# The expert loop of an audio-tower kernel: one run over all three shares instead of one run per share

## The reference

```
logits = xf @ Wr + br                       # xf: 8064 x 64, 64 experts
topk_logits, topk_idx = top_k(logits, 2)
gates = softmax(topk_logits)
for e in range(64):
    h = relu(xf @ W1[e] + b1[e])            # 64 -> 128
    y = h @ W2[e] + b2[e]                   # 128 -> 64
    out = out + combine[:, e:e+1] * y       # combine: the gates, 0 for other experts
```

## Time and profile before

| | us |
|---|---|
| median of 3 runs | 900.72 (898.73 to 900.98) |
| the profiled execution, its own time | 901.74 |
| its span in the profile | 899.9 |
| PE busy (matrix products) | 520.3 (58%) |
| DVE busy | 571.1 (63%) |
| ACT busy | 330.5 (37%) |
| POOL busy | 595.1 (66%) |
| expert loop, first to last y_copy | 524.2 to 793.3 |

### The profile page before, as it was taken

The page is one execution under the profiler, slowest core; times in us unless marked ns, Lnnn a source line. Parts: engine busy times, 40 slices in busy tenths (PEclk is TensorE's granted clock), DMA queues, the critical chain, the costliest instruction groups (busy, mean ns, idle before and its releaser), DMA issues.

```text
span 899.9 us, 9083 instructions
## 1 busy us (share of the span) xinstructions
PE 520.3 (58%) x2514; PEld 348.0 (39%) x2520; DVE 571.1 (63%) x1180; ACT 330.5 (37%) x622; POOL 595.1 (66%) x393
## 2 busy tenths in 40 slices
PE   4653344675576666667357578868767678720050
PEld 4643111221222222234234367747656567610050
DVE  1697899999999999978256623323223223284258
ACT  2169756466556555433113123323222223200020
POOL 5894699999999999913644645635655365557700
PEclk9857578798887797877568788988998799975575
DMA  7999900000000000000350257776876678211102
GB/s 245 383 160 119 48 1 0 0 0 0 0 1 0 0 0 0 0 0 23 86 142 15 69 162 223 196 206 193 230 212 183 185 213 233 59 41 27 26 1 92
DMA packets 106605, 84.96 MB, mean 94 GB/s; under 512 B 30464, under 2 KB 90240, under 8 KB 106560
## 3 DMA queue, kind: packets, MB, share of 16 engines
q1 hardware_dynamic: 79312, 54.76, 28.2%
q10 hardware_dynamic: 19184, 21.40, 7.7%
q0 software_dynamic: 8064, 8.27, 3.6%
HBM read 57.22 MB, written 33.49 MB: 101 GB/s over the span
## 4 chain that ended last, share of the span: by engine, by line
PE 27%; DVE 26%; issue 16%; POOL 13%; ACT 8%; another core or an unknown queue 8%; SPq 1%; DMA 1%; POOLq 0%; DVEq 0%; ACTq 0%
PE ps L907 11%; POOL x_w L576 7%; POOL w_ring L569 6%; PE ps L894 5%; DVE hh_ring L1422 4%; DVE x_w L1616 2%; DVE hh_ring L1633 2%; PE ps L672 2%; ACT ps L1067 2%; DVE x_w L1606 2%; DVE w_ring L1416 2%; ACT ps L1073 2%; PE ps L736 2%; DVE us_lg L1633 2%
## 5 line engine op out<-in xcount | busy, mean ns | idle before, releaser
L736 PE MATMUL ps<-x_w,ident 128*128 128x512 f32 x252 | 151.6, 760 | 102.5 <-POOL x_w L576 102.5
L626 POOL DMA_INDIRECT sorted_rows<-xp,slot_i x126 | 122.0, 968 | 124.2 <-DVE x_w L1616 42.9
L647 POOL DMA_INDIRECT xt<-expert_out,slot_i x126 | 119.9, 952 | 91.0 <-DVE x_w L1616 52.2
L569 POOL TENSOR_TENSOR w_ring<-xt,bc 128x2016 f32<-128x2016 f32 x32 | 144.7, 4522 | 13.5 <-DVE hh_ring L1422 7.3
L1422 DVE TENSOR_TENSOR_SCAN hh_ring<-ps,w_ring 128x1024 f32<-128x1024 f32 x64 | 145.6, 2275 | 0.1
L576 POOL TENSOR_TENSOR x_w<-hh_ring,bc 128x2016 f32<-128x2016 f32 (+1 forms) x32 | 142.4, 4454 | 0.9 <-PE ps L736 0.9
L736 PEld LDWEIGHTS ps<-x_w,ident 128*128 128x128 f32 x252 | 59.2, 245 | 197.7 <-POOL x_w L576 125.8
L1616 DVE COPY x_w<-ps 128x256 f32<-128x256 f32 x80 | 33.9, 424 | 128.4 <-PE ps L907 63.6
L1073 ACT ACTIVATE ps<-dt_t,a_exp 128x1024 f32<-128x1024 f32 x64 | 71.5, 1117 | 64.2 <-DVE hh_ring L1422 64.2
L1067 ACT ACTIVATE ps<-dt_t,a_exp 128x1024 f32<-128x1024 f32 x64 | 71.5, 1118 | 52.1 <-DVE w_ring L1401 52.1
L1164 ACT ACTIVATE x_w<-ps 128x256 f32<-128x256 f32 x80 | 30.6, 383 | 156.4 <-PE ps L883 95.6
(11 more groups left out here) (209 smaller groups left out, 915.8 us busy)
## 6 DMA issues: line engine op xcount, KB each, us to landing
dt_t<-packed SPq DMA_DIRECT2D x140, 96.5 KB
x_w<-packed SPq DMA_DIRECT2D x112, 96.5 KB
x_w<-sorted_rows ACTq DMA_DIRECT2D x40, 256.0 KB
expert_out<-x_w ACTq DMA_DIRECT2D x80, 128.0 KB
sorted_rows<-pad_rows SPq DMA_DIRECT2D x2, 3584.0 KB, 24.1
bc<-packed SPq DMA_DIRECT2D x68, 96.5 KB
packed<-in_L_ffn_W SPq DMA_DIRECT2D x3, 2048.0 KB, 38.7
x_w<-in_x SPq DMA_DIRECT2D x7, 448.0 KB, 9.7
```

The source lines that it names most:

```text
L569: pool.tensor_tensor(w_buf(k, 2), up3[:, bass.ds(c * DC, DC), 1:S].unsqueeze(1).broadcast_to([P, 2, DC, L]), vec_of(k, 2), ALU.mult).then_ ...
L626: pool.indirect_dma_start(out=sorted_rows[h], out_offset=bass.IndirectOffsetOnAxis(ap=slot_i[:, c, l:l + 1], axis=0), in_=xn[:, l, :], in_ ...
L647: pool.indirect_dma_start(out=y[:, l, :], out_offset=None, in_=expert_out[h], in_offset=bass.IndirectOffsetOnAxis(ap=slot_i[:, c, l:l + 1] ...
L736: ins = pe.matmul(ps[:, i, :], ident[:, :], src[:, i * BANK:(i + 1) * BANK], start=(k < 0), stop=(k == (N - 2 if last else N - 1)), skip_g ...
```

## The change

PE, ACT and DVE run through steps 0 to 79 in one loop. `rows_T` and `hidden` of the next share's first steps are now issued during the last steps of the share before. ACT no longer waits at the head of a share: the wait for `s_disp[h]` is in `rows_of_unit(u)`, ahead of the load of the share's first unit, and that load is now issued by `next_rows` three units ahead, as within a share. So the wait for `s_disp[1]` stands behind `xT_copy(17)` and that for `s_disp[2]` behind `xT_copy(45)`. SP, POOL and all numbers of `SHARES`, rings and `STEP_AT` stay as they are.

```diff
--- PE
-            for h in range(len(SHARES)):
-                a, z = STEP0[h], STEP0[h + 1]
-                rows_T(a)
-                rows_T(a + 1)
-                hidden(a)
-                for i in range(a, z):
-                    if i + 2 < z:
-                        rows_T(i + 2)
-                    if i + 1 < z:
-                        hidden(i + 1)
-                    outputs(i)
+            rows_T(0)
+            rows_T(1)
+            hidden(0)
+            for i in range(STEP0[-1]):
+                if i + 2 < STEP0[-1]:
+                    rows_T(i + 2)
+                if i + 1 < STEP0[-1]:
+                    hidden(i + 1)
+                outputs(i)
--- ACT
+            def rows_of_unit(u):
+
+                if u in UNIT0:
+                    h = UNIT0.index(u)
+                    act.wait_ge(s_disp[h], 16 * 2 * (SHARES[h][1] - SHARES[h][0]))
+                load_rows(act, u)
+
             def next_rows(i):
 
-                h = share_at(STEP0, i)
-                d = i - STEP0[h] + 1
+                d = i + 1
                 u = d // (UNIT // 2) - 1 + RING
-                if d % (UNIT // 2) == 0 and u < UNITS[h]:
-                    load_rows(act, UNIT0[h] + u)
-
-            for h in range(len(SHARES)):
-                a, z = STEP0[h], STEP0[h + 1]
-                act.wait_ge(s_disp[h], 16 * 2 * (SHARES[h][1] - SHARES[h][0]))
-                for v in range(RING):
-                    load_rows(act, UNIT0[h] + v)
-                for i in range(a, a + 2):
-                    xT_copy(i)
-                    next_rows(i)
-                relu_A(a)
-                for i in range(a, z):
-                    if i + 2 < z:
-                        xT_copy(i + 2)
-                        next_rows(i + 2)
-                    if i + 1 < z:
-                        relu_A(i + 1)
-                    if i > a:
-                        store(i - 1)
-                store(z - 1)
+                if d % (UNIT // 2) == 0 and u < UNIT0[-1]:
+                    rows_of_unit(u)
+
+            for v in range(RING):
+                rows_of_unit(v)
+            for i in range(2):
+                xT_copy(i)
+                next_rows(i)
+            relu_A(0)
+            for i in range(STEP0[-1]):
+                if i + 2 < STEP0[-1]:
+                    xT_copy(i + 2)
+                    next_rows(i + 2)
+                if i + 1 < STEP0[-1]:
+                    relu_A(i + 1)
+                if i > 0:
+                    store(i - 1)
+            store(STEP0[-1] - 1)
--- DVE
-            for h in range(len(SHARES)):
-                a, z = STEP0[h], STEP0[h + 1]
-                relu_B(a)
-                for i in range(a, z):
-                    if i + 1 < z:
-                        relu_B(i + 1)
-                    y_copy(i)
+            relu_B(0)
+            for i in range(STEP0[-1]):
+                if i + 1 < STEP0[-1]:
+                    relu_B(i + 1)
+                y_copy(i)
```

## The result

The changed kernel takes 885.05 us (882.56 to 888.75, 4 runs) where the kernel before takes 899.73 (898.38 to 900.98, 4 runs): 14.7 us less, ratio 0.984, 95% interval 0.980 to 0.988. The forecast was 882.3 us in a range of 878.5 to 888.5; the measured time lies in that range, but just above the narrower one that the forecast had for itself, 881 to 884.5. The profiled execution took 885.48 us, 16.3 less than that of before, against 18.4 forecast; that of before had been 2.0 us above its median, this one is 0.4 above.

The account below looks back on a forecast made before the run. No engine held over 27% of the span; the chain passed between engines. Two drains, 25.1 us, less 6.3 to 7.0 for ordinary intervals, saved 18.4: median 900.72 to 882.3 us, range 878.5 to 888.5, its own 881 to 884.5.

Parts of the forecast that it names:

- Two drains go: Between shares 0, 1 and 2: the two gaps, 25.1 us together, become ordinary intervals; 18.1 to 18.8 us saved, 18.4 taken.
- Fill at a low clock: Inside a drain the pipeline refills with PE at 1.2 GHz much of the time; the first eight output products take 2.93 us.
- released by the first load: At a share's head PE waits for the first load of rows, landing 4.7 us after ACT issues the loads.
- The ordinary interval: Two intervals between `y_copy` replacing the drains: 6.3 us at the shares' mean, or 7.0 as bare steps plus five indirect DMAs.
- the part behind the loop: From the last `y_copy` to the end: order unchanged, gathers start 2.6 us behind it, and these 106 us move as a whole.
- the loop's bare chain: Output products, `y_copy`, next products, without POOL's bursts: 2.22 us a step, read from the last two `y_copy`.
- 0.51 us for each indirect DMA: In the shares: excess of 73.1 us over bare steps, counted as the price of each of 144 indirect DMAs beside the loop.
- The scatters' wait, moved ahead,: ACT's wait behind `xT_copy(17)` and `xT_copy(45)`: last scatters out 10.1 and 25.4 us before, so it costs nothing.
- Rival A: Bursts from the drains cost nothing beside steps: two new intervals take 4.4 us, 20.7 us saved, 880.0 us; chance 0.15.
- Rival B: Steps get slower without the pauses, all at share 1's 3.25 us: loop 256.6 us, 12.5 saved, 888.2 us; chance 0.15.
- Rival C: Share 1's scatters land so late that ACT stands behind `xT_copy(17)`: slower than before, 907.2 us at 35 us landing; chance 0.02.
- Rival D: POOL, not the loop, sets the end and only idles less: no change, 900.7 us; chance 0.02.

## Why the prediction was right, and where its size was off

**Two drains go** (25.1 us for two ordinary steps): right. They went to 4.18 and 3.66 us in the first profile, and each alone was worth its gap less one step where it was tried, 10.4 and 10.5 us, on a chip without the waits of the first session.

**"Fill at a low clock", "released by the first load":** right, and the run with the loads ahead shows how it divides. I had put the loads at 4.7 us and held the rest for the fill. At the first boundary (13.28 us there) the later start was 6.3 us and the clock, which goes with it, about 2.3; the draining itself was 2.3 and a step 2.4.

**The ordinary interval** is the term that was mis-sized, and the part behind the loop hid more than half of the error. I took the intervals of the shares as they were and set 6.3 to 7.0 us for the two new ones. They took 7.8, and the others grew by 3.7 us: 1.6 at the end of share 0, whose last steps had been cheap because the pipeline ran dry beside them, and most of the rest in the burst behind the store of step 51. I had named that wait and given it "about 1 us at worst", with a store that lands 2.6 us after its `y_copy`. That figure came from the end of the loop, where nothing stands ahead of the store; in the middle it was issued 1.65 us after it and landed 5.7 us after its `y_copy`. POOL waited 3.23 us, and what cost the loop was not the wait but the six gathers in a row behind it. The 2.22 us that I called the loop's bare chain came from the loop's end too; the later traces have 2.37 in its middle. So two of the signs that I had set failed: the loop is 255.5 us long and not 250 to 251, and one interval is over 6 us. The mean interval, 3.23 us, stayed within its bounds. The part behind the loop, which I held constant, gave 3.3 us back: that is luck, and without it the saving in the profile would have been 13.0 us and not 16.3, against 18.4.

**0.51 us for each indirect DMA**: a count of what the first trace held (with a bare step of 2.37 us it would have been 0.43), not a price of the kernel. The loop keeps 2.37 us a step with none, some or all of the gathers beside it. What remains is that in the session of the first traces ACT and DVE stopped beside POOL's bursts, and PE behind them.

**The scatters' wait, moved ahead,** costs nothing: no interval near steps 15 and 43 stands out in any trace, as the sum had it. ACT stood 2.18 and 2.87 us before these two `xT_copy` in the first profile, no longer than beside other bursts (up to 3.06). The landing of a scatter is still in no row, and the Trainium skill's 2.1 us (page "DMA: Bandwidth & Descriptors", section "Anatomy of one DMA — SWDGE (gpsimd) path") was not tested.

**Rival A** (bursts cost nothing, 880.0) has the mechanism right where the waits of the first session are absent: the two gaps give 25.4 - 4.7 = 20.6 us there, and the loop is 20.4 us shorter, near its 20.7. The Trainium skill's rule (page "SBUF — State Buffer", section "Who interferes with whom"), that ACT waits for nobody's port, agrees with these later traces, where ACT has no wait without a named releaser beside any burst. What held ACT in the first traces was not shown; DVE's 9.50 us of waiting for its own increments speak for something other than a port. **Rival B** (slower steps, 888.2) had the right sign for what the first profile shows; it had named late stores, bursts that fall badly and DMA load. The store of step 51 and its burst fit the first two. DMA load alone does not slow a step: in a later session steps take 2.37 us at a DMA share of 1.01. **Rival C** never came near. **Rival D** (POOL sets the end) did not come true either, since the end moved with the loop; but POOL's slack is down to 2 us.

## What to carry to other kernels

A pipeline that drains at a block's end pays for the fill's slowest input first: look at what the first instruction of the fill waits for, since issuing the next block's loads ahead gave 15.5 of 17.1 us here. Do not take a store's landing from the end of a loop for one in its middle, where other work of its engine stands ahead of the issue: here 5.7 us behind its `y_copy` and not 2.6. Price an interval from the steady middle, not from a mean that holds the cheap steps in front of a drain. And ask how much the engine that runs beside the loop has left before cutting the loop further; here 2 us.

## What the runs showed of the hardware

The same kernel takes 900 us in one session and 776 us in the others, and the traces part only behind POOL's first indirect DMA. In the first session ACT and DVE stop together, mostly for 2 to 3 us, beside bursts of four and for 4.5 beside six, the last of DVE's instructions with an increment each come 1.4 us apart instead of 0.23, and DVE waits 5.3 and 9.5 us for its own increments. That reads as semaphore updates held up while indirect DMAs run, but it was not shown: no trace of the later sessions has it, and what the sessions differ in stays open. The change helps in both, by 14.7 and by 17 to 19 us.

An indirect DMA of 128 rows of 256 bytes keeps POOL busy for 0.95 to 0.97 us, and 0.30 us lie between two: 1.26 us each, beside the loop and behind it. Eight output products took 2.93 us at the low clock, behind a pause of PE of 6.17 us, and 1.57 us where the loads ahead had cut that pause.
